# Q projected before K in each head pair of a fused attention and FFN layer

## The chip, the cores and the metric

The kernel runs as one program on the eight cores of one Trainium2 chip. The metric is the device time in microseconds (us) of the slowest core. Each core has the engines TensorE (PE in the rows, with its weight loads as PEld), VectorE (DVE), ScalarE (ACT), GpSimd (POOL) and SyncE (SP), which issues most of the DMAs. Two kernels are told apart from about 2% of their time.

## The reference

The input X is 4 x 2048 x 2048. It is normalized to xn and goes through an attention branch and a quantized FFN branch; their outputs and X are added.

```python
xn = _layernorm(x)
x = x + _L0_attn_ref(xn, ...) + _L0_ffn_ref(xn, ...)
# in _L0_attn_ref, 16 heads of 128:
Xn  = layernorm(X) * ln_w + ln_b          # a second layernorm, of xn
Q, K, V = split(Xn @ W_in)                # W_in 2048 x 6144
Q, K = rope(Q), rope(K)                   # first 64 channels of a head
out = softmax(Q @ K.T / sqrt(128)) @ V @ W_out + X
# in _L0_ffn_ref: silu(h @ Wg.T) * (h @ Wu.T) @ Wd.T, weights dequantized, 8192 wide
```

## The kernel before

Each core takes one batch element and one half of its query rows: it computes K and V for all 2048 rows of the batch element, but Q, the output projection and the FFN for 1024 rows.

The program is written as a list of operations in program order (`Prog.op`, `Prog.dma`). Each engine executes its own operations in that order, and an operation waits on semaphores for the values given with it. Nothing reorders the operations afterwards.

The stages are these.

- `_emit_ln` (lines 240 to 376): 16 row tiles of X are loaded, normalized twice on VectorE, ScalarE and GpSimd, and transposed on TensorE (L343) into `xn2` (2048 rows, bf16, called `xn2f` in the rows) and `xnfm`. The last transposes end the stage; their sequence number is kept as `p1T`.
- `_emit_attention`: a loop over eight groups `g` of two heads. A group needs three weight slabs of W_in, in this order of number: 3g for Q, 3g+1 for K, 3g+2 for V. `load_slab(j)` (L438, L444) brings one slab in eight pieces of 128x512 float32, through the two staging buffers `wf32` (rows: `wf`), each cast by GpSimd into the bf16 buffer `wbf[j % 3]`. So Q always lies in `wbf0`, K in `wbf1`, V in `wbf2`. The cast of a slab's first piece waits for the last matmul that read that buffer. Slabs 0, 1 and 2 are requested at the start of the stage and wait there for `p1T`; slabs 3g+3 to 3g+5 are requested in the program behind group g's V projection.
- In a group come first the twelve Q and K jobs (`qk_jobs`): eight for K (two heads, four blocks of 512 rows) and four for Q (two heads, two blocks). A job is 16 matmuls of 128x512 (L476) into one of the four PSUM tiles `pp0`, `pp1`, `ppC0`, `ppC1` in turn, and a ScalarE copy (L483) into `k2` or `q2`. Behind the matmuls of the next job stands the rotary step `rope` of the job before: a 64x512 matmul into `ppR` (L497) and three VectorE operations (L501, L505, L508). The last job's rope stands directly behind the one before it.
- Then come 16 V tiles (L611), between them the steps `bsteps` that find a bound for the softmax from the squares of Q and K (L537, L541 on ScalarE, L552 and L583 on TensorE, L558 to L586 on VectorE).
- Then the attention of the group, four units of 16 key blocks: scores (L651), exponential (L662), context and denominator (L669 to L697), reciprocal and product (L702, L705).
- `_emit_outproj` (L802), and `_emit_ffn` (L922, L940, L952, L995), which also writes the output.

The first matmul of a job waits for its slab and for its PSUM tile. In group 0 it waits besides for the transposed row tiles of its block:

```python
w0 = [("gpsimd", slab_ready[slabj])] + pp_free[sl] + k2_rd
if g == 0:
    w0 += env["x2ev"][4 * tg + 3]
if g == 0 and tile_i in (2, 3):
    w0 += env["x2ev"][14] + env["x2ev"][15]
k2_rd = []
```

`k2_rd` holds the last readers of `k2` and `q2` in the group before; only the first job waits for them.

Of the kernel before, what the change touches and what calls it, by code (L numbers as in the profile page):

```python
# [115 lines left out]
def build_program(stage=STAGE, debug=DEBUG):  # L116
# [45 lines left out]
    with ExitStack() as top:  # L162
# [23 lines left out]
        with ExitStack() as sCtx:  # L186
          env["sCtx"] = sCtx
          with ExitStack() as sA:
            env["xn2"] = sA.enter_context(nc.sbuf_tensor("xn2f", [128, ND * S], BF16, side="left"))
            env["cs"] = sA.enter_context(nc.sbuf_tensor("cs_sb", [128, S], F32, side="left"))  # L190
            ldc = []
            for i, (name, dst) in enumerate([
                    ("lnwc", env["lnw"]), ("lnbc", env["lnb"]),
                    ("gscp", env["gsc"]), ("uscp", env["usc"]),
                    ("pmat", env["pm"]), ("idf", env["idf"]),
                    ("cs", env["cs"])]):
                prog.dma("sync", lambda e, d=dst, s=dram[name]: e.dma_start(out=d[:, :], in_=s[:, :]),
                         sem=f"ldc{i}")
                ldc.append((f"ldc{i}", 16))
            env["ldc"] = ldc  # L200
            for dst, valc in [(env["ones_cb"], 1.0), (env["ones_bb"], 1.0), (env["ones_rf"], 1.0),
                              (env["n128"], -128.0), (env["eps_c"], EPS)]:
                prog.op("vector", lambda e, d=dst, vv=valc: e.memset(d[:, :], vv))
            env["dvc_done"] = prog.v("vector")

            _emit_ln(env, xb)
            if debug:
                prog.barrier()
                prog.dma("sync", lambda e: e.dma_start(out=dram["d_xn2"][:, :], in_=env["xn2"][:, :]), sem="st")
                prog.dma("sync", lambda e: e.dma_start(out=dram["d_xnfm"][:, :], in_=env["xnfm"][:, :]), sem="st")  # L210
                prog.dma("sync", lambda e: e.dma_start(out=dram["d_rstd"][:, :], in_=env["rstd"][:, :]), sem="st")
                prog.dma("sync", lambda e: e.dma_start(out=dram["d_nmr"][:, :], in_=env["nmr"][:, :]), sem="st")

            if stage >= 2:
                _emit_attention(env)
                if stage == 2:
                    prog.barrier()
# [167 lines left out]
def _emit_attention(env):  # L385
# [12 lines left out]
    with ExitStack() as ctx:  # L398
# [56 lines left out]
        for g in range(8):  # L455
# [1 line left out]
            rope_last = 0  # L457
            vproj_last = 0
            rope_done = {}
            qk_jobs = [("k", hh, tg) for hh in range(2) for tg in range(4)] + \  # L460
                      [("q", hh, tg) for hh in range(2) for tg in range(2)]
            pending_rope = None
            for kind, hh, tg in qk_jobs:
                slabj = 3 * g + (0 if kind == "q" else 1)
# [718 lines left out]
```

How the kernel before makes its waits and increments, by code:

```python
            def body(eng):  # L89
                for fn, waits, eseq, dsem in ops:
                    if fn == "BARRIER":
                        if e == "sync":
                            eng.sem_inc(sems["bar"], 1)
                        else:
                            eng.drain().then_inc(sems["bar"], 1)
                        eng.wait_ge(sems["bar"], waits)
                        continue
                    for wname, wval in waits:
                        if wname in ENGS:
                            eng.wait_ge(sems["q" + wname], rank[wname][wval])
                        else:
                            eng.wait_ge(sems[wname], wval)
                    inst = fn(eng)
                    if dsem is not None:
                        inst.then_inc(sems[dsem], 16)
                    if eseq in marks:
                        inst.then_inc(sems["q" + e], 1)
```

## Time and profile before

| | us |
|---|---|
| median of the two runs | 3111.64 |
| lowest, highest run | 2981.55, 3241.73 |
| profiled execution | 2982.16 |
| span of its slowest core (core 7), first to last instruction | 2980.6 |
| span of its fastest core (core 5) | 2964.1 |

The profiled execution is 1.56 us longer than the span of core 7. Unless a row names another core, it is of core 7. A row with "x16" stands for 16 instructions; the duration of a group of matmuls runs from the start of the first to the modelled end of the last. An entry in brackets tells how long the engine was idle before the row, and what released it.

### The profile page before, as it was taken

The numbers are of one execution on the slowest core, as the hardware profiler recorded it, in microseconds if no ns is written. First come the engines' busy times: TensorE is split into PE (matmuls) and PEld (weight loads), VectorE is DVE, ScalarE is ACT, GpSimd is POOL, SyncE is SP. The second block draws the span as 40 slices with busy tenths as digits, with TensorE's granted clock in tenths as the row PEclk, the third lists the DMA queues.
The fourth block names the chain that finished last, engine by engine and source line by source line (L and its number), as shares of the span: only waits on it lengthen the run. The fifth ranks groups of instructions, "written<-read, shape, count | busy, mean of one in ns | idle before, by whom it ended". The sixth has DMA issues, their size and how long they took to land.

```text
span 2980.6 us, 37395 instructions; the slowest of 8 cores (2964.1 to 2980.6 us)
## 1 busy us (share of the span) xinstructions
PE 2600.6 (87%) x12552; PEld 1247.7 (42%) x12552; DVE 635.6 (21%) x1044; ACT 815.7 (27%) x1330; POOL 386.7 (13%) x388
## 2 busy tenths in 40 slices
PE   4445898989889898985979999989997999998996
PEld 2222545444444445452434444434443444443443
DVE  5752243424242433333100000000110000000111
ACT  5571345352616262634111111110001111110000
POOL 2241202010110101000001111110001111110010
PEclk9757999999999999997989999999998999999998
DMA  4113202021111101002314333434544333433553
GB/s 130 57 57 92 86 1 86 16 70 33 54 51 36 57 29 57 22 1 85 141 72 154 142 141 150 161 126 146 198 169 152 141 142 147 159 147 117 175 181 120
DMA packets 64491, 305.61 MB, mean 103 GB/s; under 512 B 7732, under 2 KB 7860, under 8 KB 40632
## 3 DMA queue, kind: packets, MB, share of 16 engines
q1 hardware_dynamic: 55096, 286.45, 27.1%
q10 hardware_dynamic: 9216, 16.78, 1.7%
q8 instruction: 112, 1.84, 0.3%
q14 instruction: 67, 0.55, 0.1%
HBM read 294.81 MB, written 8.39 MB: 102 GB/s over the span
## 4 chain that ended last, share of the span: by engine, by line
PE 85%; DMA 4%; issue 3%; DVE 3%; ACT 2%; POOL 1%; ACTq 0%; SPq 0%; DVEq 0%; POOLq 0%
PE pg L922 15%; PE pu L940 15%; PE pg L995 8%; PE pu L995 7%; PE pp L476 6%; PE ppC L476 6%; PE ppC L611 4%; PE po L802 4%; PE pp L611 4%; PE ppC L669 3%; PE ppD L677 3%; PE pst L343 3%; PE pp L651 2%; PE ppR L497 1%; PE ppR L651 1%
## 5 line engine op out<-in xcount | busy, mean ns | idle before, releaser
L922 PE MATMUL pg<-xnfm,wstage 128*128 128x512 bf16 x2048 | 466.7, 381 | 19.8 <-ACT sgp L931 12.9
L940 PE MATMUL pu<-xnfm,wstage 128*128 128x512 bf16 x2048 | 464.6, 380 | 2.4 <-DMA wstage<-ubp 2.4
L922 PEld LDWEIGHTS pg<-xnfm,wstage 128*128 128x128 bf16 x2048 | 201.1, 98 | 265.8 <-issue 26.9
L952 POOL TENSOR_TENSOR hfm<-sgp,sup 128x512 bf16<-128x512 f32 x128 | 161.7, 1263 | 1109.7 <-ACT sup L948 1109.7
L940 PEld LDWEIGHTS pu<-xnfm,wstage 128*128 128x128 bf16 x2048 | 200.7, 98 | 245.6 <-issue 5.1
L931 ACT ACTIVATE sgp<-pg,gsc_sb 128x512 f32<-128x512 f32 x128 | 87.9, 687 | 615.9 <-PE pg L922 344.9
L995 PE MATMUL pg<-wstage,hfm 128*128 128x512 bf16 x1024 | 232.9, 385 | 15.3 <-DMA wstage<-dwp 15.3
L662 ACT ACTIVATE ebig<-pp,biasc 128x512 bf16<-128x512 f32 x344 | 228.8, 686 | 30.7 <-PE pp L651 27.6
L444 POOL CAST wbf<-wf 128x512 bf16<-128x512 f32 x192 | 120.6, 632 | 873.0 <-PE ppC L476 518.4
L995 PE MATMUL pu<-wstage,hfm 128*128 128x512 bf16 x1024 | 227.7, 379 | 0.0
L476 PE MATMUL pp<-xn2f,wbf 128*128 128x512 bf16 x768 | 174.4, 382 | 32.2 <-POOL wbf L444 31.9
L972 DVE CAST hsr<-phs 1x512 bf16<-1x512 f32 x2 | 1.4, 678 | 914.4 <-PE phs L961 914.4
L669 PE MATMUL ppC<-ebig,v 128*128 128x512 bf16 x448 | 169.6, 379 | 27.0 <-ACT ebig L662 26.9
L948 ACT ACTIVATE sup<-pu,usc_sb 128x512 f32<-128x512 f32 x128 | 87.9, 687 | 374.1 <-PE pu L940 374.1
L343 PE MATMUL pst<-idf_sb,xn2t 128*128 128x128 f32 x256 | 70.5, 390 | 124.9 <-POOL xn2t L320 124.7
L702 DVE RECIPROCAL rb<-ppD 128x512 f32<-128x512 f32 x32 | 107.4, 3358 | 323.2 <-PE pp L651 185.0
L476 PE MATMUL ppC<-xn2f,wbf 128*128 128x512 bf16 x768 | 174.1, 380 | 0.0
L677 PE MATMUL ppD<-ebig,ones_bb 128*128 128x512 bf16 x448 | 169.7, 379 | 0.0
L995 PEld LDWEIGHTS pg<-wstage,hfm 128*128 128x128 bf16 x1024 | 100.1, 99 | 140.1 <-issue 26.0
L995 PEld LDWEIGHTS pu<-wstage,hfm 128*128 128x128 bf16 x1024 | 98.9, 98 | 120.7 <-issue 3.6
L802 PE MATMUL po<-wob,ctxf 128*128 128x512 bf16 x512 | 112.7, 384 | 28.7 <-DVE wob L786 28.7
L611 PE MATMUL pp<-wbf,xn2f 128*128 128x256 bf16 x1024 | 132.6, 289 | 0.2
(105 smaller groups left out, 2267.1 us busy)
## 6 DMA issues: line engine op xcount, KB each, us to landing
wstage<-gbp SPq DMA_DIRECT2D x64, 1024.0 KB, 4.9
wstage<-ubp SPq DMA_DIRECT2D x64, 1024.0 KB, 7.0
wstage<-dwp SPq DMA_DIRECT2D x32, 2048.0 KB, 9.0
wf<-wip SPq DMA_DIRECT2D x192, 256.0 KB, 2.9
xt<-xb SPq DMA_DIRECT2D x16, 1024.0 KB, 9.2
wof<-wop SPq DMA_DIRECT2D x8, 2048.0 KB, 9.8
xst<-xb ACTq DMA_DIRECT2D x32, 256.0 KB, 6.0
out<-out_acc ACTq DMA_DIRECT2D x32, 256.0 KB, 3.6
```

Source lines behind the costliest of these rows:

```text
L343: mm_t = prog.op(T, lambda e, sb=srcbuf, d=dc, pp=p: e.transpose(pp[:, 0:128], sb[:, d * 128:(d + 1) * 128], idf[:, :]), waits=wts)
L444: cv = prog.op("gpsimd", lambda e, jj=j, h=qt, q=qp: e.tensor_copy(wbf[jj % 3][:, h * 512:(h + 1) * 512], wf32[q][:, :]), waits=wts)
L476: m_last = prog.op(T, lambda e, d=dc, h=hh, t=tg, s=sl, sj=slabj: e.matmul(pp4[s][:, :], wbf[sj % 3][:, d * 256 + h * 128: d * 256 + (h + ...
L611: m_last = prog.op(T, lambda e, d=dc, t=tb, s=sl, sj=slabv: e.matmul(pp4[s][:, 0:256], xn2f[:, d * S + t * 128: d * S + t * 128 + 128], wb ...
L662: ex_seq[kb] = prog.op(Sc, lambda e, k=kb, s=sl, h=hh: e.activation(ebig[:, (k % 8) * 512:(k % 8) * 512 + 512], pps[s][:, :], AF.Exp, bias ...
L669: prog.op(T, lambda e, k=kb - 2, h=hh, u=un: e.matmul(ppC[u][:, :], v2[:, k * 256 + h * 128: k * 256 + (h + 1) * 128], ebig[:, (k % 8) * 5 ...
L677: md_seq[kb - 2] = prog.op(T, lambda e, k=kb - 2, u=un: e.matmul(ppD[u][:, :], ones_bb[:, :], ebig[:, (k % 8) * 512:(k % 8) * 512 + 512], ...
L802: m_last = prog.op(T, lambda e, hh=h, t=tb, s=sl, q=wp: e.matmul(po[s][:, :], ctxf[:, hh * 1024 + t * 128: hh * 1024 + (t + 1) * 128], wob ...
L922: m = prog.op(T, lambda e, h=hc, i2=ic2, p=par, t=tg, s=psl: e.matmul(pg[s][:, :], gb2[p][:, h * 256 + i2 * 128: h * 256 + i2 * 128 + 128] ...
L940: m = prog.op(T, lambda e, h=hc, i2=ic2, p=par, t=tg, s=psl: e.matmul(pu[s][:, :], ub2[p][:, h * 256 + i2 * 128: h * 256 + i2 * 128 + 128] ...
L952: gh = prog.op(G, lambda e, i=ic: e.tensor_mul(hfm[:, i * 512:(i + 1) * 512], sgp[:, :], sup[:, :]), waits=[(Sc, a2), (Sc, a1), (T, h_free)])
L995: m = prog.op(T, lambda e, f=fg, p=pc, q=par, t=tb, i=icp: e.matmul(pd[t][:, :], hfm[:, (p * 16 + i) * 512 + t * 128: (p * 16 + i) * 512 + ...
```

## The change

The list of the twelve Q and K jobs is turned round: the four Q jobs stand ahead of the eight K jobs, in each of the eight groups. The order of the slab loads stays as it was (Q, K, V), and so do all operations, their sizes and their number.

```diff
@@ -457,8 +457,8 @@
             rope_last = 0
             vproj_last = 0
             rope_done = {}
-            qk_jobs = [("k", hh, tg) for hh in range(2) for tg in range(4)] + \
-                      [("q", hh, tg) for hh in range(2) for tg in range(2)]
+            qk_jobs = [("q", hh, tg) for hh in range(2) for tg in range(2)] + \
+                      [("k", hh, tg) for hh in range(2) for tg in range(4)]
             pending_rope = None
             for kind, hh, tg in qk_jobs:
                 slabj = 3 * g + (0 if kind == "q" else 1)
```

On TensorE, at the start of group 0 behind the last transposes (L343), the program now has this order; `wbf0` is the Q slab and `wbf1` the K slab:

```order
 L343 MATMUL pst3<-idf_sb,xn2t3 128x128
+L476 MATMUL pp0<-xn2f,wbf0 128x512 x16
+L476 MATMUL pp1<-xn2f,wbf0 128x512 x16
+L497 MATMUL ppR<-q2,pm_sb 64x512
+L476 MATMUL ppC0<-xn2f,wbf0 128x512 x16
+L497 MATMUL ppR<-q2,pm_sb 64x512
+L476 MATMUL ppC1<-xn2f,wbf0 128x512 x16
+L497 MATMUL ppR<-q2,pm_sb 64x512
 L476 MATMUL pp0<-xn2f,wbf1 128x512 x16
```

The four jobs that read `wbf0` have moved ahead of the first job that reads `wbf1`.

At the end of the same twelve jobs, TensorE's order ahead of the V projection (L611, from `wbf2`) is now:

```order
 L476 MATMUL ppC1<-xn2f,wbf1 128x512 x16
-L497 MATMUL ppR<-k2,pm_sb 64x512
-L476 MATMUL pp0<-xn2f,wbf0 128x512 x16
-L497 MATMUL ppR<-k2,pm_sb 64x512
-L476 MATMUL pp1<-xn2f,wbf0 128x512 x16
-L497 MATMUL ppR<-q2,pm_sb 64x512
-L476 MATMUL ppC0<-xn2f,wbf0 128x512 x16
-L497 MATMUL ppR<-q2,pm_sb 64x512
-L476 MATMUL ppC1<-xn2f,wbf0 128x512 x16
-L497 MATMUL ppR<-q2,pm_sb 64x512 x2
+L497 MATMUL ppR<-k2,pm_sb 64x512 x2
 L611 MATMUL pp0<-wbf2,xn2f 128x256 x16
```

The last reader of `wbf0` stood directly ahead of the V projection; now the last reader of `wbf1` does. The two rope matmuls at the end are of K instead of Q. GpSimd and SyncE have the same operations in the same order in both programs; on GpSimd the casts of the first slabs stand so:

```order
44 L444 CAST wbf0<-wf32_1 128x512 [waits ldw1]
45 L444 CAST wbf1<-wf32_0 128x512 [waits ldw0]
...
60 L444 CAST wbf2<-wf32_1 128x512 [waits ldw1]
61 L444 CAST wbf0<-wf32_0 128x512 [waits ldw0,qtensor]
...
69 L444 CAST wbf1<-wf32_0 128x512 [waits ldw0,qtensor]
```

The first casts of the slabs for group 1 (the rows with `qtensor`) wait for TensorE: the first for the last Q job, the second for the last K job of group 0.

## Rows read from the trace of the kernel before

**Rows 1.** Span and mean granted clock of the fastest and the slowest core.

```profile
core 5: 2964.1 us, clock 0.957
...
core 7: 2980.6 us, clock 0.948
```

**Rows 2.** The page, part 4: chain that ended last, shares by engine.

```profile
PE 85%; DMA 4%; issue 3%; DVE 3%; ACT 2%; POOL 1%; ACTq 0%; SPq 0%; DVEq 0%; POOLq 0%
```

**Rows 3.** Waits of PE over the span: us in total, times, longest.

```profile
PE pst L343 <- POOL xn2t L320: 124.7, 4, 43.2
PE pp L476 <- POOL wbf L444: 31.9, 1, 31.9
...
PE ppR L497 <- DVE rb L505: 14.2, 8, 1.8
```

**Rows 4.** PE in order of time, start of group 0 to its V projection.

```profile
258.39 8.89 PE L476 MATMUL pp<-xn2f,wbf 128*128 128x512 bf16 x32 [31.92 <-POOL wbf L444]
...
275.32 3.63 PE L476 MATMUL pp<-xn2f,wbf 128*128 128x512 bf16 x16
...
306.11 0.40 PE L497 MATMUL ppR<-q,pm_sb 64*64 64x512 bf16 x1
308.31 0.37 PE L497 MATMUL ppR<-q,pm_sb 64*64 64x512 bf16 x1 [1.80 <-DVE rb L505]
```

**Rows 5.** POOL in order of time: last casts of slabs 0, 1, 2; first of 3.

```profile
241.77 0.61 POOL L444 CAST wbf<-wf 128x512 bf16<-128x512 f32 x1 [0.54 <-DMA wf<-wip]
...
257.38 0.61 POOL L444 CAST wbf<-wf 128x512 bf16<-128x512 f32 x1 [0.90 <-DMA wf<-wip]
...
272.27 0.61 POOL L444 CAST wbf<-wf 128x512 bf16<-128x512 f32 x1 [0.61 <-DMA wf<-wip]
306.31 1.63 POOL L444 CAST wbf<-wf 128x512 bf16<-128x512 f32 x2 [33.43 <-PE ppC L476]
```

**Rows 6.** Stretches around the first matmuls: us, busy per engine, granted clock, DMA share, GB/s.

```profile
240.00:258.00 18.00, 0.00 (x0) 0.00 (x0) 0.00 (x0) 0.00 (x0) 6.13 (x10) 0.50 0.46 134
258.00:262.00 4.00, 3.61 (x9) 1.31 (x10) 0.00 (x0) 0.00 (x0) 1.23 (x2) 0.50 0.47 134
262.00:280.00 18.00, 18.00 (x80) 7.41 (x79) 6.83 (x10) 2.98 (x5) 3.68 (x6) 1.00 0.37 114
```

**Rows 7.** POOL of cores 3 and 6: slab 0's and slab 1's last casts.

```profile
240.11 0.61 POOL L444 CAST wbf<-wf 128x512 bf16<-128x512 f32 x1 [0.52 <-DMA wf<-wip]
...
256.25 0.61 POOL L444 CAST wbf<-wf 128x512 bf16<-128x512 f32 x1 [1.34 <-DMA wf<-wip]
...
244.17 0.61 POOL L444 CAST wbf<-wf 128x512 bf16<-128x512 f32 x1 [1.30 <-DMA wf<-wip]
...
259.10 0.61 POOL L444 CAST wbf<-wf 128x512 bf16<-128x512 f32 x1 [1.04 <-DMA wf<-wip]
```

**Rows 8.** PE of core 5: the first two jobs of group 0.

```profile
256.20 9.96 PE L476 MATMUL pp<-xn2f,wbf 128*128 128x512 bf16 x32 [31.73 <-POOL wbf L444]
```

**Rows 9.** Chain in order of time: first two jobs of groups 0 to 3.

```profile
258.39 8.89 PE pp L476 x32
...
402.65 7.07 PE pp L476 x32
...
540.21 7.07 PE pp L476 x32
...
682.39 7.07 PE pp L476 x32
```

**Rows 10.** Waits of POOL over the span: us in total, times, longest.

```profile
POOL wbf L444 <- PE ppC L476: 518.4, 7, 81.8
```

**Rows 11.** DVE in order of time: rope operations of group 0.

```profile
302.73 0.68 DVE L501 TENSOR_TENSOR q<-q,cs_sb 64x512 bf16<-64x512 bf16 x1 [1.72 <-PE ppR L497]
...
306.62 0.85 DVE L501 TENSOR_TENSOR q<-q,cs_sb 64x512 bf16<-64x512 bf16 x1 [1.72 <-PE ppR L497]
```

**Rows 12.** Stretches in the V projections of group 0, then of group 1.

```profile
328.00:338.00 10.00, 7.45 (x37) 5.32 (x37) 1.72 (x8) 1.83 (x4) 1.85 (x3) 0.66 0.37 112
...
470.00:480.00 10.00, 6.96 (x58) 5.57 (x59) 2.46 (x8) 3.04 (x5) 2.45 (x4) 1.00 0.39 125
```

## The prediction

> **What bounds the kernel now.** I read the cores first: core 7 ends last at 2980.6 us, core 5 first at 2964.1 [rows 1]. The profiled execution took 2982.16 us, which is 1.56 us more than core 7's span. It agrees within 0.6 us with the lower of the two runs shown (2981.55); the median of 3111.64 is the mean of that one and one of 3241.73. My sum is made against the profiled execution and forecasts an execution like it.
>
> The chain that ended last is TensorE for 85% of the span [rows 2], so what counts is a moment in which TensorE waits. The change touches only the Q and K jobs, so I look in the waits of PE for those that belong to them. There are two. L476 waits for the casts of the weight slabs exactly once, 31.9 us; L497 (the rope matmul) waits for L505 eight times, 14.2 us, once in each group [rows 3]. The largest wait, 124.7 us for the normalization, lies ahead of the change.
>
> In order of time the wait of 31.92 us ends at 258.39, at the first K job of group 0 [rows 4]. GpSimd shows why it is so long. The last cast of slab 0 (Q) ends at 241.77 + 0.61 = 242.38, that of slab 1 (K) at 257.38 + 0.61 = 257.99, that of slab 2 (V) at 272.27 + 0.61 = 272.88 [rows 5]. TensorE starts 258.39 - 257.99 = 0.40 behind the K slab. So while it waited, the Q slab lay ready from 242.38 on, and no Q job stood in front of the queue.
>
> In groups 1 to 7 there is no such wait [rows 3]. On the contrary, GpSimd waits seven times for a matmul of L476 to free a buffer, 518.4 us in all [rows 10]: it has the slabs long before they are read.
>
> **The change, part by part.**
>
> *Group 0, start.* The first matmul now reads slab 0. It can start at 242.38 + 0.40 = 242.78 in place of 258.39, so 15.61 us earlier, if the other conditions hold by then: the transposed row tiles do (the slab loads themselves wait for the last transpose), and the PSUM tiles were not in use.
>
> *Group 0, the step from Q to K.* The fifth job now needs slab 1. Before, the fifth job started at 275.32, which is 16.93 us behind the first [rows 4]. After the change it comes at 242.78 + 16.93 = 259.71. Slab 1 is usable at 257.99 + 0.40 = 258.39. That leaves a margin of 1.32 us, if the loads keep their pace. I take the same pace: the 15.61 us of slab 1 fell in a stretch in which TensorE was idle, and the 272.88 - 257.99 = 14.89 us of slab 2 in one in which it worked, with 10 VectorE operations beside it [rows 5, 6]. Working engines did not slow the loads. So no new wait, and the whole 15.61 us stay.
>
> *The clock.* In the 18 us before the first matmul the granted clock was at 0.50 of full speed, that is 1.2 GHz; it stayed there in the first stretch of work, 258 to 262, and stood at 1.00 (2.4 GHz) from 262 on [rows 6]. The idle stretch shrinks from 31.9 to 31.9 - 15.6 = 16.3 us and stays idle, so I let the four first jobs begin at 1.2 GHz as now and take the same 16.93 us. Bounds: the first two jobs took 8.89 us on core 7, 9.96 on core 5 [rows 4, 8], and 7.07 at the full clock in the later groups [rows 9]. A later rise costs up to 9.96 - 8.89 = 1.1 us. An immediate rise gives at most 8.89 - 7.07 = 1.8 us, but then the fifth job would be ready before its slab: its start can't be earlier than 258.39, and the gain ends at 275.32 - 258.39 = 16.93 us, 1.3 more than my value.
>
> *Other cores.* The gap between the two slabs is the gain: 256.25 - 240.11 = 16.14 us on core 3, 259.10 - 244.17 = 14.93 us on core 6, the largest and the smallest of the eight [rows 7]. The core that ends last gains about the same as core 7.
>
> *V slab of group 0.* The V projection, which now follows the rope matmul of 308.31, moves to about 308.7 - 15.6 = 293 [rows 4]; its slab lies ready at 272.88 [rows 5]. Cover of 20 us.
>
> *Groups 1 to 7.* Each job costs the same in either order, the PSUM tiles rotate as before, and the first job waits for the same last readers. No gain.
>
> *Reloading the slabs.* The first cast of the next Q slab started at 306.31, just behind the last Q job [rows 5]. In group 0 it can now follow slab 2 at once, from 273 on, and its 15 us lie beside the K jobs; the next K slab then starts behind the last K job, at about 306.3 - 15.6 = 290.7. Each comes earlier, and both were early before. Nothing is issued in another order on SP or GpSimd. Cost 0, hidden by the 518 us in which GpSimd stood waiting [rows 10].
>
> *Rope beside casts.* This is what gets worse. A rope multiplication took 0.68 us with GpSimd idle and 0.85 us when it ran beside the casts that began at 306.31 [rows 5, 11]. Eight casts per group now fall beside K jobs. If each lengthened one of three VectorE operations by 0.17 us, that were 8 x 0.17 = 1.4 us of VectorE time per group, in which VectorE is idle 1.72 us ahead of every rope [rows 11]. Hidden: cost 0. The last two ropes, for which TensorE waits 1.80 us [rows 4], are followed by casts of the slab just freed, before as after. Bounds: 0 to 7 x 0.17 = 1.2 us more in that wait, or as much less.
>
> The Trainium skill, "GPSIMD Engine Reference", section "Key points", says that GpSimd shares its SBUF interfaces with VectorE and that there is contention with VectorE instructions with two SBUF inputs, which L501 and L508 are. By that rule all K ropes of a group could lose time; by the row, one lost 0.17 us. Either lies inside the 1.72 us of idle time, and the sum stays.
>
> *Sum.* 2982.16 - 15.61 = 2966.55, say 2966.5 us, 0.5% less. That is far below the 2% that a measurement of this kernel can tell from no change.
>
> **The rivals.**
>
> *1. The slab becomes late (gain lost).* The margin is 1.32 us, each us beyond it costs one. For the whole gain to go, slab 1 would need 15.61 + 1.32 + 15.61 = 32.5 us. For it speaks only that the load is now waited for by a running engine; against it stands the pace of slab 2, 14.89 us beside a working TensorE [rows 5]. At double time for the slab (31.2 us) the wait is 14.3 us and the time 2980.8: no change. A tenth slower costs 0.2 us.
>
> *2. The clock in the V projections, to the slow side.* Group 1, from its first job to that of group 2, took 540.21 - 402.65 = 137.56 us, group 2 took 682.39 - 540.21 = 142.18 [rows 9]. The work is the same; the difference of 4.6 us is the clock: in a V projection with many short waits the granted clock averaged 0.66 in a stretch of group 0, and 1.00 in the like one of group 1 [rows 12]. On core 7 long and short groups alternate. The change shifts all groups by 15.6 us, and where the drops fall may be drawn again. If the slowest core had a drop in all seven following groups in place of about half of them, 3 or 4 more, it would lose up to 4 x 4.6 = 18.4 us: 2966.5 + 18.4 = 2985, slower than before. The point from which it decides is 15.6 / 4.6 = 3.4, so four more long groups on the core that ends last. Against it: they alternate now, and it takes a systematic reason to make them all long.
>
> *3. The same, to the fast side.* Core 5 ends 16.5 us ahead of core 7 with the same work [rows 1]. If the slowest core had two long groups fewer, 2966.5 - 9.2 = 2957.
>
> *4. The change does nothing outside its order.* If the first Q job waited for something else that comes with the K slab, TensorE would start at 258.39 as before: 2982. No wait of that job names such a thing.
>
> **How the numbers follow.** Forecast, 2960 to 2973, one long group more or less: 0.70. Fast side, under 2960: 0.08. Part or all of the gain lost (rivals 1 and 4, and two or three long groups more), 2973 to 2982: 0.14. Slower than before (rival 2): 0.08. The range 2957 to 2982 leaves out about 0.12. None of the cases reaches 2% (60 us) on either side. I leave 0.02 for faster by more, since no wait of that size stands in the jobs, and 0.03 for slower by more; 0.95 for within 2%.
>
> **What would show it.** PE's wait for L444 at the first L476 should be about 16.3 us in place of 31.9, with the first matmul near 242.8 on core 7; no second wait for L444 at the fifth job, or one under 1 us; the V projection of group 0 near 293; the groups 1 to 7 at 137.6 or 142.2 us; the first cast of slab 3 near 273 and that of slab 4 near 291; K ropes in groups at 0.68 to 0.85 us. The forecast is wrong if a wait for L444 of several us stands at the fifth job, if the rope matmuls wait for L505 more than once in a group, or if the sum of the eight groups differs by more than 5 us from now.

## The result, and the profile after

| | before | after |
|---|---|---|
| median of the runs, us | 2983.13 (22 runs) | 2966.87 (24 runs) |
| ratio, 95% interval | | 0.9936, 0.9916 to 0.9956 |
| span of the slowest core of the profiled execution | 2980.6 (core 7) | 2964.6 (core 1) |
| first and last span of the eight cores | 2964.1, 2980.6 | 2949.1, 2964.6 |

The forecast was 2966.5 us. The change takes 0.64% off, which is well below 2% but clear of the interval. In some executions of either kernel the cores of one of the chip's two dies, or of both, run at a lower clock and the time reaches 3500 us; the ratios leave those out, but the medians here and below contain them (without them the table's would be 2982.9 and 2965.4).

The waits of PE of the changed kernel (core 1: us in total, times, longest), against [rows 3]:

```profile
PE pst L343 <- POOL xn2t L320: 125.9, 4, 44.4
...
PE pp L476 <- POOL wbf L444: 17.8, 1, 17.8
...
PE ppR L497 <- DVE rb L505: 14.2, 8, 1.8
```

The wait for the slab went from 31.9 us to 17.8, still once. The normalization ahead of it and the rope wait behind it are as they were. The same start in order of time, core 1, against [rows 4]:

```profile
243.06 9.58 PE L476 MATMUL pp<-xn2f,wbf 128*128 128x512 bf16 x32 [17.79 <-POOL wbf L444]
...
260.68 3.63 PE L476 MATMUL pp<-xn2f,wbf 128*128 128x512 bf16 x16
...
291.47 0.40 PE L497 MATMUL ppR<-k,pm_sb 64*64 64x512 bf16 x1
293.67 0.37 PE L497 MATMUL ppR<-k,pm_sb 64*64 64x512 bf16 x1 [1.80 <-DVE rb L505]
294.24 3.65 PE L611 MATMUL pp<-wbf,xn2f 128*128 128x256 bf16 x32 [0.21 <-issue]
```

The first row holds the first two jobs. The fifth job, the first that reads the K slab, starts at 260.68 with no wait in brackets, and so it does on the other seven cores. GpSimd on the same core, against [rows 5]:

```profile
242.00 0.61 POOL L444 CAST wbf<-wf 128x512 bf16<-128x512 f32 x1 [0.75 <-DMA wf<-wip]
...
257.88 0.61 POOL L444 CAST wbf<-wf 128x512 bf16<-128x512 f32 x1 [1.81 <-DMA wf<-wip]
...
275.85 0.61 POOL L444 CAST wbf<-wf 128x512 bf16<-128x512 f32 x1 [0.42 <-DMA wf<-wip]
...
291.68 0.61 POOL L444 CAST wbf<-wf 128x512 bf16<-128x512 f32 x1 [0.58 <-PE ppC L476]
```

The first two rows end slab 0 at 242.61 and slab 1 at 258.49, 15.88 us apart. TensorE starts 0.45 behind slab 0, and the K slab is usable at 258.94, 1.74 us ahead of need. Over the eight cores this margin goes from 0.3 us (core 4) to 2.8 us (core 7), and the slabs lie 14.5 to 16.4 us apart. The third row is the first cast of the next Q slab, 30 us earlier than in [rows 5], which are of core 7; the fourth is the first cast of the next K slab, which waits for the last K job.

### The profile page after: what moved, and what is told of

Its sections match the earlier page's. It is cut to its first block, busy times and chain, and to the rows that moved or that the text cites. A ratio compares the mean times of both kernels' runs of the same rounds, so it can differ in the third digit from the quotient of the medians.

```text
span 2964.6 us, 37395 instructions; the slowest of 8 cores (2949.1 to 2964.6 us)
## 1 busy us (share of the span) xinstructions
PE 2599.7 (88%) x12552; PEld 1244.3 (42%) x12552; DVE 636.3 (21%) x1044; ACT 815.6 (28%) x1330; POOL 390.8 (13%) x388
## 3 DMA queue, kind: packets, MB, share of 16 engines
q1 hardware_dynamic: 55096, 286.45, 27.5%
## 4 chain that ended last, share of the span: by engine, by line
PE 85%; DMA 4%; issue 4%; DVE 3%; ACT 2%; POOL 1%; ACTq 0%; SPq 0%; DVEq 0%; POOLq 0%
PE pg L922 15%; PE pu L940 15%; PE pg L995 8%; PE pu L995 8%; PE pp L476 6%; PE ppC L476 6%; PE ppC L611 4%; PE pp L611 4%; PE po L802 4%; PE ppC L669 3%; PE ppD L677 3%; PE pst L343 3%; PE pp L651 2%; PE ppR L497 1%; PE ppR L651 1%
## 5 line engine op out<-in xcount | busy, mean ns | idle before, releaser
L662 ACT ACTIVATE ebig<-pp,biasc 128x512 bf16<-128x512 f32 x344 | 228.8, 686 | 30.7 <-PE pp L651 27.5
L476 PE MATMUL pp<-xn2f,wbf 128*128 128x512 bf16 x768 | 175.1, 383 | 18.1 <-POOL wbf L444 17.8
L343 PE MATMUL pst<-idf_sb,xn2t 128*128 128x128 f32 x256 | 68.0, 355 | 126.2 <-POOL xn2t L320 125.9
L476 PE MATMUL ppC<-xn2f,wbf 128*128 128x512 bf16 x768 | 174.1, 380 | 0.0
L995 PEld LDWEIGHTS pg<-wstage,hfm 128*128 128x128 bf16 x1024 | 100.0, 99 | 139.9 <-issue 25.6
L611 PE MATMUL pp<-wbf,xn2f 128*128 128x256 bf16 x1024 | 133.8, 290 | 0.6 <-issue 0.4
```

What stands on the lines that cost most here:

```text
L343: mm_t = prog.op(T, lambda e, sb=srcbuf, d=dc, pp=p: e.transpose(pp[:, 0:128], sb[:, d * 128:(d + 1) * 128], idf[:, :]), waits=wts)
L476: m_last = prog.op(T, lambda e, d=dc, h=hh, t=tg, s=sl, sj=slabj: e.matmul(pp4[s][:, :], wbf[sj % 3][:, d * 256 + h * 128: d * 256 + (h + ...
L611: m_last = prog.op(T, lambda e, d=dc, t=tb, s=sl, sj=slabv: e.matmul(pp4[s][:, 0:256], xn2f[:, d * S + t * 128: d * S + t * 128 + 128], wb ...
L662: ex_seq[kb] = prog.op(Sc, lambda e, k=kb, s=sl, h=hh: e.activation(ebig[:, (k % 8) * 512:(k % 8) * 512 + 512], pps[s][:, :], AF.Exp, bias ...
L995: m = prog.op(T, lambda e, f=fg, p=pc, q=par, t=tb, i=icp: e.matmul(pd[t][:, :], hfm[:, (p * 16 + i) * 512 + t * 128: (p * 16 + i) * 512 + ...
```

## The experiments

The first four kernels take the change apart; the ratios are to the kernel before, run on the same chip.

**K first, K slab first.** From the kernel before:

```diff
-        load_slab(0)
         load_slab(1)
+        load_slab(0)
         load_slab(2)
```

Expected: 

> The jobs stand as in the kernel before (K first, then Q); only the first three slabs are loaded in the order K, Q, V in place of Q, K, V. Theory (the gain is the wait for one slab in place of two at the start of group 0, whichever slab it is): TensorE's wait for L444 at its first L476 falls from 31.9 to about 16 us, the eight K jobs (some 32 us) cover the Q slab, no second wait; time near 2967 us, ratio about 0.994 to the kernel before. Rival (the gain comes from running Q first: fewer jobs before the K reload, other places of casts and ropes in all groups): no gain from the load order alone beyond the start, so if it carries the gain, time near 2983, ratio 1.00.

Measured: 2965.45 us, ratio 0.9945 (0.9924 to 0.9966). TensorE's wait (core 5, the slowest):

```profile
PE pp L476 <- POOL wbf L444: 16.0, 1, 16.0
```

The same gain comes without moving a single matmul. What counts is that the first job and the first slab belong together, not that the job is of Q; the Q slab, now the second, is waited for on no core.

**Q first in group 0 alone.** In the changed kernel, `if g > 0:` the K jobs are put ahead again.

Expected: 

> Q jobs first in group 0 only; groups 1 to 7 run K first as in the kernel before. Theory: the whole gain is in group 0, so time near 2967 us, ratio about 0.994; the clock pattern of the groups may be drawn again, a few us either way. Rival (part of the gain, or a loss that hides a larger one, is in groups 1 to 7): time off 2967 by more than 5 us.

Measured: 2966.43 us, ratio 0.9949 (0.9929 to 0.9969). The whole gain is in group 0.

**Q first in groups 1 to 7 alone.** The same with `if g == 0:`.

Expected: 

> K jobs first in group 0, Q first in groups 1 to 7: the other half of the change. Theory: first L476 waits 31.9 us as before, time near 2983 us, ratio 1.00. Rival (later groups gain by the earlier slab reload or another clock pattern): ratio below 0.998. If the group lengths change from 137.6 and 142.2 us to 139 and 141 as they did with the whole change, the order of the jobs sets that pattern; if they stay, the shift in time of the groups does.

Measured: 2981.99 us, ratio 0.9998 (0.9988 to 1.0009). The other seven eighths of the edit are worth nothing, within 0.12% or 4 us either way. The second question of this run, what sets the lengths of the single groups, stays open. In the chain in order of time, groups 1 to 5 of its core 3 begin here (three added lines make L476 to L479):

```profile
400.43 7.07 PE pp L479 x32
537.70 7.07 PE pp L479 x32
678.30 7.07 PE pp L479 x32
817.44 7.07 PE pp L479 x32
958.13 7.07 PE pp L479 x32
```

and in the kernel with K first and the K slab first (its core 0), where the jobs stand as before and only the start is earlier, here:

```profile
386.26 7.07 PE pp L476 x32
524.02 7.07 PE pp L476 x32
665.96 7.07 PE pp L476 x32
803.84 7.07 PE pp L476 x32
945.90 7.07 PE pp L476 x32
```

With Q first the groups take 137.3, 140.6, 139.1 and 140.7 us, with K first 137.8, 141.9, 137.9 and 142.1, as in [rows 9]. But these are two cores, and other cores of both kernels show mixtures. The runs below decide against the order as the cause: with K first and four staging buffers, core 0 has the lengths that Q first has here, and with Q first and the K slab last, core 5 has 137.2, 137.4, 142.2 and 137.6 us. The order alone doesn't set the pattern. What holds in all these kernels is the average: 139.4 and 139.9 us over these four groups, and 138.5 to 140.2 us over groups 1 to 6, whichever core and kernel with the rope wait in place is taken.

**The K slab last.** The changed kernel with the loads in the order Q, V, K.

Expected: 

> The changed kernel (Q first) with the first three slabs loaded in the order Q, V, K, so that the K slab is ready some 15 us later. Prices rival 1 of the prediction. Theory: TensorE starts as early as in the changed kernel (near 243) and then waits about 14 us at the fifth job, since the margin there is about 1.3 us in the trace of before; the V slab is early and gives nothing; time near 2967 + 14 = 2981 us, ratio about 0.999. Rival (the margin is larger, or a second wait costs less than its length because the rest of group 0 was waiting anyway): clearly under 2978.

Measured: 2982.85 us, ratio 0.9999 (0.9988 to 1.0011). PE in order of time, core 2, the slowest:

```profile
242.34 8.79 PE L476 MATMUL pp<-xn2f,wbf 128*128 128x512 bf16 x31 [17.14 <-POOL wbf L444]
...
274.44 6.54 PE L476 MATMUL pp<-xn2f,wbf 128*128 128x512 bf16 x16 [15.20 <-POOL wbf L444]
```

Rival 1 at full price: the K slab comes one slab time late, TensorE waits 10.6 to 15.2 us on the eight cores, and the gain is gone. The wait is not all: the job behind it took 6.54 us in place of 3.63. The clock had fallen by the end of the wait, as the stretch behind it shows (columns as in [rows 6]; granted clock 0.50):

```profile
274.00:278.00 4.00, 3.56 (x9) 1.31 (x10) 0.00 (x0) 0.00 (x0) 1.23 (x2) 0.50 0.47 133
```

On the other cores that job took 4.96 to 6.34 us. So a second wait of this size costs its length and 1.3 to 2.9 us of restart.

The next five ask what the start of group 0 is bound by once Q is first.

**Following the pieces.** `load_slab` notes each cast (`piece_ready[(j, qt)] = cv`), and in group 0 batches of four jobs run together, each on its own PSUM tile:

```diff
+            batches = [qk_jobs[0:4], qk_jobs[4:8]] + [[j] for j in qk_jobs[8:]] \
+                if g == 0 else [[j] for j in qk_jobs]
...
+                for qt in range(8):
+                    for it in info:
...
+                        for dc in (2 * qt, 2 * qt + 1):
+                            wts = ()
+                            if dc == 2 * qt:
+                                wts = [("gpsimd", piece_ready[(slabj, qt)])]
```

The ropes of a batch are collected and issued two behind each later job.

Expected: 

> From the changed kernel: in group 0 the four Q jobs run together, two matmuls of each behind each of the eight pieces of the Q slab, and so do the first four K jobs behind the pieces of the K slab; the other four K jobs and groups 1 to 7 stay. Theory (TensorE's start is bound by the supply of slabs, 15 us each, not by its own work): the Q jobs end about 2 us behind the Q slab, near 244, the first K jobs near 260, the last four K jobs near 275, where the V slab has just come; the V projection starts near 275 in place of 293, time near 2967 - 18 = 2949 us, ratio about 0.989. Rival (the two matmuls per job in turn, a cold clock or the bunched ropes cost what is won): V projection not before 285, time over 2959.

Measured: 2965.69 us, ratio 0.9926 (0.9905 to 0.9947): 3 us better than the plain change by the ratios, whose intervals overlap, and not 18. The expectation fell, and its rival came true: the V projection starts at 285.5 to 290.1 on the eight cores. PE on core 3, the slowest:

```profile
262.08 0.40 PE L469 MATMUL ppR<-q,pm_sb 64*64 64x512 bf16 x1
262.41 3.63 PE L515 MATMUL pp<-xn2f,wbf 128*128 128x512 bf16 x16
265.97 0.40 PE L469 MATMUL ppR<-k,pm_sb 64*64 64x512 bf16 x1
268.00 0.37 PE L469 MATMUL ppR<-k,pm_sb 64*64 64x512 bf16 x1 [1.63 <-DVE rb L477]
268.44 5.30 PE L515 MATMUL pp<-xn2f,wbf 128*128 128x512 bf16 x16
...
289.87 3.65 PE L625 MATMUL pp<-wbf,xn2f 128*128 128x256 bf16 x32
```

The pieces did their part: eight jobs were done at 262.08, where the plain change had done four at 260.7. Then the remaining four jobs took 27.5 us (262.41 to 289.87) in place of about 15.6. Two ropes behind each job make TensorE wait 1.63 us for VectorE, four times, and the clock fell in between (the granted clock averaged 0.72 from 268 to 274 us), so that two of the four jobs took 5.30 us. The time that VectorE needs for a rope was free with one rope per job, the distance that the kernel had, and not with two; the last run below shows it from the other side.

**Pieces for Q alone.** The same kernel, with batches only for the four Q jobs.

Expected: 

> As the run with both, but only the four Q jobs follow the pieces; the eight K jobs run one behind the other and each waits for all it needs of the K slab piece by piece. Theory (behind the Q jobs the K slab is next, only 1.3 us ahead of need): the Q jobs end near 244, about 14 us early, and nearly all of that becomes a wait for the K pieces; the first K job ends with the slab near 258.5, 4 to 5 us earlier than in the changed kernel, so time near 2962 us, ratio about 0.993. Rival (Q early is worth its 14 us): time near 2953.

Measured: 2972.22 us, ratio 0.9954 (0.9936 to 0.9971): not 5 us faster than the plain change, but by the ratios, whose intervals overlap, 5 us slower. PE on core 6, the slowest:

```profile
248.44 0.59 PE L515 MATMUL pp<-xn2f,wbf 128*128 128x512 bf16 x2 [1.85 <-POOL wbf L445]
250.04 0.59 PE L515 MATMUL pp<-xn2f,wbf 128*128 128x512 bf16 x2 [1.01 <-POOL wbf L445]
252.06 1.01 PE L515 MATMUL pp<-xn2f,wbf 128*128 128x512 bf16 x2 [1.43 <-POOL wbf L445]
```

After the early Q jobs TensorE ran behind the K pieces, two matmuls to a wait. Their duration rose from 0.59 to 1.01 us: the clock fell again, to a granted 0.50 from 252 to 258 us. With that and the bunched ropes the V projection began at 297.1 to 300.0 on the eight cores, later than the 291.3 to 294.2 of the plain change. Being early only to wait again gained nothing here; what the waits and what the bunched ropes cost was not separated.

**Pieces with four staging buffers.** The kernel with pieces for Q and the first K jobs, and the edit of the next run.

Expected: 

> Both: pieces for Q and the first K jobs, and four staging buffers. Theory (if the staging sets the slab's time): slabs at 10 us are faster than TensorE's own work of 15 to 17 us for four jobs, so TensorE becomes the bound from about 230 on: the twelve jobs take about 12 x 3.9 + 2 to 4 for the cold clock, the V projection starts near 275 to 280, time about as with the pieces alone (2945 to 2952). Rival (bandwidth sets it): exactly the time of the pieces alone.

Measured: 2962.22 us, ratio 0.9919 (0.9899 to 0.9938), V projection from 286.3 to 291.1. The number expected was wrong for the same reason as above, the ropes: on core 3 TensorE again waits 1.63 to 1.80 us four times, and two of the last four jobs take 5.30 us. The time is that of the pieces alone, as the rival had it, but not for the rival's reason, since the next run shows that the slabs do come faster. The statement that TensorE's own work would be the bound is supported by the last run below.

**Four staging buffers.** The changed kernel with

```diff
-        wf32 = [R(f"wf32_{i}", [128, 512], F32) for i in range(2)]
+        wf32 = [R(f"wf32_{i}", [128, 512], F32) for i in range(4)]
...
-                qp = (j * 8 + qt) % 2
+                qp = (j * 8 + qt) % 4
```

Expected: 

> The changed kernel with four staging buffers for the float32 pieces in place of two (4 KB more per partition), nothing else. Asks what sets the 15.6 us of a slab. Theory (two buffers in turn: a landing of about 2.9 us and a cast of 0.6 us per pair of pieces, so the round trip sets it, not the bandwidth at 134 GB/s): a slab in about 10 us, the first Q job near 238, still no wait at the fifth job, time near 2967 - 5 = 2962 us or a little less. Rival (the eight cores' shared memory traffic sets it): a slab stays at 15 us or above, time unchanged at 2967.

Four runs, from 2959.8 to 3434.06 us, gave no ratio; the profiled one took 2959.8. So it ran again, with the counterpart.

Expected: 

> The changed kernel with four staging buffers once more, since too few runs of it could be compared: 2961 to 2963 us, ratio 0.993 or less, and 10 to 11 us under the kernel before with four buffers. The rival of that run (16 us in itself) expects the same difference as with two buffers, 16 us.

Measured: 2961.5 us, ratio 0.9930 (0.9917 to 0.9943). The stretches of both kernels, first the plain change (core 1), then four buffers (core 6); columns as in [rows 6]:

```profile
232.00:258.00 26.00, 14.94 (x56) 5.98 (x57) 3.07 (x5) 1.79 (x3) 8.57 (x14) 0.69 0.46 134
```

```profile
232.00:250.00 18.00, 11.94 (x45) 4.80 (x46) 2.13 (x3) 1.19 (x2) 8.01 (x13) 0.71 0.86 212
```

The DMA engines' share went from 0.46 to 0.86, and the traffic from 134 to 212 GB/s. The two staging buffers had set the pace, not the memory. The first two slabs lie 8.8 to 11.9 us apart on the eight cores, where it was 14.5 to 16.4. The wait for the first slab was 13.0 us.

**The kernel before with four staging buffers.** The same edit.

Expected: 

> The kernel before (K first) with four staging buffers. The trace of the changed kernel with four buffers had slabs 10 to 11 us apart in place of 15 to 16. Theory (Q first is worth the time of one slab load at the start of group 0, whatever sets it): here the first K job starts at about 249 in place of 258, time near 2983 - 9 = 2973 us, and Q first on top of it is worth 10 to 11 us (2961 to 2963), no longer 16. Rival (Q first is worth 16 us in itself): time here near 2978.

Measured: ratio 0.9969 (0.9956 to 0.9982), 2974.62 us in the profiled execution, with its wait on core 4, the slowest:

```profile
PE pp L476 <- POOL wbf L444: 25.6, 1, 25.6
```

Its first K job starts at 245.7 to 251.8 on the eight cores. Against it Q first is worth 0.9969 - 0.9930 = 0.0039, or 11.6 us of 2981, where it was worth 0.0064 with two buffers, or 19 us by the ratio and 16.3 by the medians. The intervals of these ratios are some 4 to 6 us to either side, so the times alone don't settle it. The starts in the traces do: on average over the eight cores, Q first brings the first job forward by 15.9 us with two buffers (258.4 to 242.5) and by 10.6 us with four (249.2 to 238.6). The gain is the time of one slab, whatever sets that time.

Groups 1 to 5 of core 0 of this run begin here:

```profile
393.69 7.07 PE pp L476 x32
530.95 7.07 PE pp L476 x32
671.60 7.07 PE pp L476 x32
810.82 7.07 PE pp L476 x32
951.50 7.07 PE pp L476 x32
```

With K first they take 137.3, 140.6, 139.2 and 140.7 us, the lengths that core 3 has above with Q first in groups 1 to 7.

The last two follow what the runs with pieces pointed at.

**The last rope behind the first V tile.** In the changed kernel the final `pending_rope()` moves from behind the job loop to behind the eviction of the first V tile:

```diff
-            if pending_rope is not None:
-                pending_rope()
-                pending_rope = None
...
                 tile_i += 1
+                if pending_rope is not None:
+                    pending_rope()
+                    pending_rope = None
```

Expected: 

> The changed kernel with the last rope of each group behind the first V tile in place of behind the rope before it. Theory (the wait of L497 for L505, 1.8 us in each of eight groups, is on the path): the 14.2 us of that wait go and the V projection starts some 2.2 us earlier in each group, time near 2967 - 8 x 2 = 2951 us, less if the clock falls in other places; ratio near 0.989. Rival (the wait comes back as another in the V projection, or the clock averages the group to 140 us whatever the waits): time over 2962.

Measured: 2946.69 us, ratio 0.9881 (0.9864 to 0.9898). PE on core 2, the slowest, at the end of group 0's jobs:

```profile
292.21 0.40 PE L497 MATMUL ppR<-k,pm_sb 64*64 64x512 bf16 x1
292.54 1.92 PE L607 MATMUL pp<-wbf,xn2f 128*128 128x256 bf16 x16
294.49 0.37 PE L497 MATMUL ppR<-k,pm_sb 64*64 64x512 bf16 x1
```

The 1.80 us are gone from every group. The gain over the plain change is 0.9936 - 0.9881 = 0.0055, 16 us by the ratios and 20 by the medians, about as much as the change itself and a little more than the 14.2 us of the wait. On core 1 seven groups took 1199.54 - 242.81 = 956.7 us, against 1223.20 - 243.06 = 980.1 on core 1 of the changed kernel, 3.3 us less per group; on average over the eight cores it is 2.7 us less. The step itself accounts for some 2 us: the V projection starts 0.33 us behind the last rope but one (292.21 to 292.54) and not 2.77 (291.47 to 294.24), and the last rope takes some 0.5 us between the V tiles. The rest was not traced. The chain rows of core 1:

```profile
242.81 8.51 PE pp L476 x32
...
1199.54 7.07 PE pp L476 x32
```

**All together.** Pieces, four buffers, and the ropes one behind each later K job and the rest behind V tiles; the edit against the kernel with pieces and four staging buffers:

```diff
                 if len(batch) == 1:
-                    for _ in range(2):
-                        if len(pending_ropes) > 1:
-                            pending_ropes.pop(0)()
-            for f in pending_ropes:
-                f()
-            pending_ropes.clear()
+                    if len(pending_ropes) > 1:
+                        pending_ropes.pop(0)()
...
                 tile_i += 1
+                if pending_ropes:
+                    pending_ropes.pop(0)()
```

Expected: 

> Pieces for the Q and the first K jobs of group 0, four staging buffers, and the ropes spread: one behind each later K job, the rest behind V tiles, in all groups. In the runs with pieces TensorE computed without a gap from 231 to 262, and then lost some 12 us to bunched ropes (4 waits of 1.6 us, and a clock that fell between them). Theory: the twelve jobs take 12 x 3.5 + 1.3 + 2 to 3 for the cold clock, so the V projection of group 0 starts near 277 in place of 289, and groups 1 to 7 gain 2 us each: time near 2967 - 16 - 14 = 2937 us, ratio near 0.984. Rival (as for the last rope alone: the waits come back): 2950 or more.

Measured: 2936.15 us, ratio 0.9839 (0.9826 to 0.9852). PE on core 3, the slowest:

```profile
277.70 0.40 PE L469 MATMUL ppR<-k,pm_sb 64*64 64x512 bf16 x1
278.03 1.92 PE L621 MATMUL pp<-wbf,xn2f 128*128 128x256 bf16 x16
```

The V projection starts at 278.03 (275.6 to 280.0 on the eight cores), against 294.24 after the plain change, and TensorE waits for a rope once in the whole span, 0.2 us. It beats both kernels, by 1.6% and 1.0%.

## Why the prediction was right, point by point

- *Start of group 0.* Forecast near 242.8 on core 7 with a wait of 16.3 us; measured 240.51 there, where the transposes had ended 2.3 us earlier (224.18 in place of 226.47), with a wait of 16.33, and 243.06 on core 1. The wait by itself varies with the end of the transposes; the gap between the slabs, on which the term rests, was forecast at 15.61 us and came out at 15.88 on core 1 and 15.6 on average over the eight cores.
- *From Q to K.* Forecast margin 1.32 us, no wait; measured 1.74 on core 1, 0.3 to 2.8 over the eight cores, no wait on any. On core 4 it was nearly used up, so that there was no wait at all is in part luck. The run with the K slab last shows that this margin decided: with the slab 10.6 to 15.2 us past it the whole gain was gone, and a restart at the low clock was added.
- *Clock at the start.* Taken as before, 8.89 us for the first two jobs; measured 9.58 on core 1, inside the bound of 9.96, and 9.21 on core 7. A slower start stretches the margin and costs as much, on core 1 0.7 us.
- *Groups 1 to 7.* Forecast 0, measured 0.9998 with an interval of a tenth of a per cent. The forecast expected single groups to stay at 137.6 or 142.2 us; on most cores they did not. On core 1 they took 138.9, 140.8, 139.1, 140.7 us:

```profile
383.99 7.07 PE pp L476 x32
522.86 7.07 PE pp L476 x32
663.68 7.07 PE pp L476 x32
802.80 7.07 PE pp L476 x32
943.49 7.07 PE pp L476 x32
```

  So the check of the prediction on group lengths failed while the sum held. Rivals 2 and 3 assumed that the long groups could add up on one core. No kernel of this study with the rope wait in place showed it: on every core the average over groups 1 to 6 lies between 138.5 and 140.2 us. Rival 3 also took the 16.5 us between cores 5 and 7 of the kernel before for long groups. But group 7 begins there at 1235.53 and 1242.33, 6.8 us apart, of which 2.2 were there at the first job; the larger part of the difference arises behind it.
- *Rope beside casts.* Forecast at 0.17 us for a multiplication beside a cast. The groups of rows by form of the changed kernel, with rows of the kernel before behind them:

```profile
L444 POOL CAST wbf<-wf 128x512 bf16<-128x512 f32 x192 | 124.6, 655 | 850.3 <-PE ppC L476 393.6 <-DMA wf<-wip 230.9 <-PE ppC L611 225.4
L501 DVE TENSOR_TENSOR k<-k,cs_sb 64x512 bf16<-64x512 bf16 x64 | 45.3, 707 | 95.1 <-PE ppR L497 94.9 <-issue 0.2
```

```profile
L444 POOL CAST wbf<-wf 128x512 bf16<-128x512 f32 x192 | 120.6, 632 | 873.0 <-PE ppC L476 518.4 <-DMA wf<-wip 219.0 <-PE ppC L611 132.2
L501 DVE TENSOR_TENSOR k<-k,cs_sb 64x512 bf16<-64x512 bf16 x64 | 43.8, 685 | 158.6 <-PE ppR L497 158.6
```

  The K ropes lost 1.5 us in all (45.3 - 43.8) and the casts 4.0 us. Single ones lost more than 0.17: the multiplication of the last rope of group 0, beside a cast, took 1.09 us. The Trainium skill, "GPSIMD Engine Reference", section "Key points", speaks of contention with VectorE instructions with two SBUF inputs; the trace agrees in direction, and all of it stayed hidden, since the rope wait is 14.2 us before and after.
- *The sum.* 2966.5 against 2966.87. That the two agree to 0.4 us is luck beyond what was known: the spans of the eight cores lie 15 us apart, the slowest was another core, and by the ratio the gain is 19 us (13 to 25) where 15.6 were forecast.

What was worked out wrong came later, in the expectations on the pieces: they counted the matmuls and the slabs and left out that the ropes, which had been hidden one per job, were bunched.

## What to carry to other kernels

When several operands arrive one after the other at the start of a stage, let the first job be one that needs only the first of them, and have at least one transfer time of such work before the second is needed: the gain is one transfer, once, and it is gone when the second comes one transfer late. A wait that appears once per loop iteration, such as a short step that follows its own producer at the end of a job list, can be worth more than its look: here 1.8 us eight times was about as much as the whole start. Jobs that run ahead move their side steps too; keep these spread; here the engine that was freed waited for them, and its clock fell besides.

## What the runs showed of the hardware that was not expected

- The float32 slab came at 134 GB/s with two staging buffers and at 212 GB/s with four, DMA share 0.46 and 0.86, while the median landing of a piece rose only from 3.0 to 3.6 us. Two more buffers of 2 KB per partition brought the time of a slab down to two thirds (10.2 us on average over the eight cores in place of 15.6).
- TensorE's clock fell in stretches in which no single wait was longer than 2 us: two K jobs at 5.30 us between bunched ropes (granted clock 0.72 from 268 to 274 us), pairs of matmuls at 1.01 in place of 0.59 us behind the K pieces (0.50 from 252 to 258 us). After a wait of 15.2 us a job took 6.54 in place of 3.63 us.
- Groups with equal work differ by up to some 5 us, and the clock differs with them: over group 1 of core 7 of the kernel before (402 to 540 us) the granted clock averaged 1.00, over group 2 (540 to 682 us) 0.96. The pattern varies from core to core within one kernel, and yet the average over groups 1 to 6 is always 138.5 to 140.2 us. When the rope wait was taken out, it fell to 136.5 to 137.7 us, on average by more than the wait. Why the sum is so steady, and what sets the pattern, was not tried.
